# A graph network's kernel on one core: the search's loads and products moved, masks of the real columns alone, two parts finished together, and another last stage

## The chip, the cores and the metric

The kernel runs on one core of one Trainium2 chip. A core has a matrix engine (PE; its weight loads are listed as PEld), a vector engine (DVE), a scalar engine (ACT), GpSimd (POOL), and SyncE (SP), which here only issues transfers. They run their own instruction streams and wait for one another on semaphores. The metric is the device time of one execution in microseconds (us); lower is better. The median of the runs shown is what the prediction is about.

## What is computed

Input: x of 2500 nodes x 256, 40000 edges sorted by destination (denser at low numbers), and the weights of four blocks, each added to its normalized input:

```python
h = max(layernorm(x), 0); x = x + gat(gat(h))       # 8 heads of 32, leaky_relu, softmax over a node's edges
h = max(layernorm(x), 0); x = x + h @ W             # W: edge weights set at [src, dst], the last one of a cell wins
h = max(layernorm(x), 0); x = x + sage_and_dense(h) # three neighbour means, three dense layers
h = max(layernorm(x), 0); x = x + elu(elu(gat4(h))) # 4 heads of 64, exp(-leaky_relu), rows and columns swapped
```

An attention head is worked as a dense product: the edges are first turned into a matrix C of counts (source x destination), and a mask "score above zero" splits C in two, so that the leaky exponential factors into two products of a row term and a column term.

## The kernel before

NT = 20 tiles of 128 nodes hold the 2500 nodes; the last 60 columns of the last tile are padding.

**The count matrix (lines 439 to 612).** The edges lie in 313 chunks of 128. For each of NW = 40 ranges of 64 destinations the chunks that reach into it are taken, in groups of U3 = 3 (387 chunks in all here; 20 ranges have only six chunks, 12 have nine, the first has 54). Per chunk DVE makes two one-hot matrices, `ohc` (line 558) and `ohl` (line 560), in a ring of three; PE multiplies them in three products into `acc` (line 596). Before a slot is used again DVE waits for `s_used`. ACT copies the finished range from `acc` to C (line 542) and prepares `near`, which DVE compares with, for the range after next (line 518). In each range there is also one step of a search for the edges of a cell that are not its last: SP loads rows of keys to `right` and `left` (lines 508, 510), PE makes two products into `psD` (lines 604, 606), ACT squares and clips them (lines 532, 536) and GpSimd scatters the weights (line 423). The body of PE for a range is: the search's products, the first three chunks, the loop over the rest. SP's program starts with nine other loads: x (2.4 MB), its tail, two weight matrices, four attention vectors, a bias (lines 493 to 499); then come the key rows, each waiting until the search before has been done.

**An attention (lines 630 to 1215; three of them).** After the projection and a preparation of factors, a loop over heads `h` and parts `p` of the destination columns makes masks and products. The first two attentions have 8 heads and 2 parts of W = 1280 columns; the third (`split`) has 4 heads and 4 parts of 640. In a part there are 20 steps `s`, one for each source tile. A step is: ACT makes `Rm` = Relu(row term + column bias) (line 1067), DVE takes M = min(Rm, C) (line 1111), PE multiplies M and C with the value matrices (lines 1198 to 1208). With two parts, every fourth step has no ACT operation: DVE compares and multiplies by itself (line 1114); the set `MORE_ON_ACT` gives one such step in each part back to ACT. With four parts, 12 of the 20 steps have a second DVE product Mn (line 1101). Rm and M are rings of SG = 4 slots (5 in the third). After LEAD steps of a part (4; 7) the part before is evacuated: ACT copies the low halves from PSUM to `tl` (line 1075), and DVE puts its stages one by one between its masks: add (line 1138), two scalings by `F2` and `F1` (1142, 1143), their sum `q1` (1147), weight (1152), inverse (1156), mean (1160), and with two parts and p = 1 a copy out of `stash` (1165).

**The last stage (`elu`, lines 1217 to 1308, called on line 2235).** Two ELUs, one on the other, over five batches of four tiles: DVE makes minimum and maximum, ACT the exponential of 1024 columns, DVE the sum, and again. GpSimd issues the load of `xr`, the residual, in one transfer (line 2225), and the output, one transfer for each batch (lines 2230, 2232).

## Time and profile before

| | us |
|---|---|
| median of 3 runs | 2196.62 (2195.84 to 2196.69) |
| the profiled execution | 2193.83 |
| its span in the trace | 2192.2 |
| stage of the count matrix | 33 to 347 |
| masks and products of attention 1 | 421 to 767 |
| of attention 2 | 842 to 1188 |
| of attention 3 | 1877 to 2150 |
| last stage, with the end | 2150 to 2192.2 |

Busy shares of the span: PE 80%, DVE 74%, ACT 64%, POOL 14%. In a row of the timeline stand the start, the duration, the engine, the line, the operation, output<-input with their shapes and count, and in brackets how long the engine stood idle before it and who released it. Rows with x2 or more are merged. Instructions of DVE and ACT overlap by some 0.09 us, so that the distance of two starts is smaller than a duration. Stages between 1188 and 1877 us (the second and third block) are not touched by the change.

### The profile page before, as it was taken

To read this page: it belongs to the slowest core of one execution; us is meant where nothing else is said; L and a number is where in the kernel's file an instruction comes from. 1 tells how busy PE (TensorE), PEld (TensorE's weight loads), DVE (VectorE), ACT (ScalarE), POOL (GpSimd) and SP (SyncE) were. 2 spreads that over 40 slices of the span, in tenths; PEclk is the share of its full clock that TensorE was granted. 3 is DMA by queue.
4 is the path that set the end of the run, shared out by engine and by line. 5 is a ranking of instruction groups with operands and counts; after the bars stand their busy time and mean duration, and the time that the engine had idled before them with its cause. 6 is when DMAs were issued, how large, how long until landed. Compare 5 with 4: busy or idle time off the path is not lost. (4 is left out here: it accounts for less than half of the span.)

```text
span 2192.2 us, 64066 instructions
## 1 busy us (share of the span) xinstructions
PE 1747.3 (80%) x21987; PEld 1343.4 (61%) x21987; DVE 1618.4 (74%) x3673; ACT 1410.0 (64%) x2346; POOL 299.0 (14%) x457
## 2 busy tenths in 40 slices
PE   2998886298998855989885499998989984688881
PEld 1333334288888735888884356665548973688881
DVE  4988877899999978999999722222332257899997
ACT  0146675799999849999996712221213355899992
POOL 2465500466400011000000000000000001000000
PEclk9999998699999987999998799999999997899996
DMA  3000000010110000101011110000001010000102
GB/s 85 1 1 2 2 2 1 27 39 26 38 38 27 14 26 16 38 27 39 26 38 35 67 42 1 0 0 7 1 21 33 22 56 13 14 20 21 27 15 95
DMA packets 32298, 54.99 MB, mean 25 GB/s; under 512 B 10541, under 2 KB 23626, under 8 KB 31800
## 3 DMA queue, kind: packets, MB, share of 16 engines
q1 hardware_dynamic: 27848, 46.45, 6.5%
q0 software_dynamic: 4208, 5.24, 0.7%
q8 instruction: 160, 2.62, 0.5%
q14 instruction: 82, 0.67, 0.1%
HBM read 43.19 MB, written 8.49 MB: 24 GB/s over the span
## 5 line engine op out<-in xcount | busy, mean ns | idle before, releaser
L1198 PE MATMUL ps<-R,M 128*128 128x132 f16 (+1 forms) x8640 | 808.8, 221 | 202.7 <-DVE M L1111 101.9
L1067 ACT ACTIVATE Rm<-rows,cB 128x1280 bf16<-128x1280 f32 (+1 forms) x832 | 884.3, 1153 | 20.3 <-DVE Mn L1101 13.8
L1198 PEld LDWEIGHTS ps<-R,M 128*128 128x128 f16 x8640 | 728.8, 97 | 245.6 <-issue 115.2
L1206 PE MATMUL ps<-HB,C 128*128 128x66 f16 x6400 | 596.1, 193 | 0.0
L1111 DVE TENSOR_TENSOR M<-Rm,C 128x1280 f16<-128x1280 bf16 (+1 forms) x832 | 555.3, 691 | 41.0 <-ACT Rm L1067 37.4
L1206 PEld LDWEIGHTS ps<-HB,C 128*128 128x128 f16 x6400 | 571.7, 97 | 0.0
L1630 PE MATMUL psA<-R,C 128*128 128x512 f16 (+1 forms) x1200 | 253.0, 350 | 20.3 <-POOL ones L1664 9.5
L558 DVE TENSOR_SCALAR ohc<-cells,near 128x1280 f16<-128x1280 f16 x387 | 213.2, 551 | 58.4 <-PE acc L596 54.8
L596 PE MATMUL acc<-ohc,ohl 128*128 128x420 f16 (+1 forms) x1161 | 244.2, 348 | 1.6 <-DVE ohl L560 0.4
L1114 DVE SCALAR_TENSOR_TENSOR M<-rows,cN,C 128x1280 f16<-128x1280 f32 x128 | 197.9, 1546 | 0.0
L1630 PEld LDWEIGHTS psA<-R,C 128*128 (+1 forms) x1200 | 118.7, 99 | 117.5 <-issue 33.2
L596 PEld LDWEIGHTS acc<-ohc,ohl 128*128 128x128 f16 x1161 | 89.9, 98 | 148.6 <-DVE ohl L560 94.1
L423 POOL DMA_INDIRECT wd<-wv,wi x104 | 123.2, 1185 | 128.3 <-issue 71.6
L542 ACT ACTIVATE C<-acc 128x420 f16<-128x420 f32 (+1 forms) x120 | 55.7, 542 | 125.0 <-PE acc L596 125.0
L1781 DVE TENSOR_SCALAR rdeg<-psD 128x1 f32 (+1 forms) x20 | 3.2, 158 | 153.0 <-ACT tl L1746 153.0
L560 DVE TENSOR_SCALAR ohl<-lows,bT 128x128 f16<-128x128 f16 x387 | 101.5, 262 | 0.0
L1560 ACT ACTIVATE R<-L 128x256 f32 (+3 forms) x40 | 14.5, 363 | 129.8 <-DVE L L1792 80.3
L1101 DVE TENSOR_TENSOR Mn<-C,M 128x640 f16<-128x640 f16 x192 | 93.5, 487 | 0.6
L1201 PE MATMUL ps<-VS,C 128*128 128x130 f16 x640 | 88.7, 222 | 0.0
L1198 PE MATMUL ps<-R,Mn 128*128 128x130 f16 x960 | 86.8, 220 | 0.0
L1754 ACT ACTIVATE hT<-ps,b0c 128x128 f32<-128x128 f32 x80 | 22.9, 368 | 86.9 <-PE ps L1705 86.9
L1705 PE MATMUL ps<-xT,W 128*128 128x128 f32 x640 | 76.3, 278 | 1.6 <-ACT xT L1750 1.6
(300 smaller groups left out, 2333.9 us busy)
## 6 DMA issues: line engine op xcount, KB each, us to landing
rows<-rowd SPq DMA_DIRECT2D x32, 640.0 KB, 3.9
rows<-rowd SPq DMA_DIRECT2D x16, 320.0 KB, 3.5
xd<-R SPq DMA_DIRECT2D x4, 640.0 KB, 2.9
xr<-xd SPq DMA_DIRECT2D x20, 128.0 KB, 2.0
xd<-HB SPq DMA_DIRECT2D x1, 2560.0 KB
xr<-xd POOLq DMA_DIRECT2D x1, 2560.0 KB, 9.2
R<-in_x SPq DMA_DIRECT2D x1, 2432.0 KB
xr<-in_x SPq DMA_DIRECT2D x19, 128.0 KB, 2.0
```

What stands on the lines that cost most here:

```text
L423: g.indirect_dma_start(out=wd[:, :], out_offset=bass.IndirectOffsetOnAxis(ap=m["wi"][w][:, :], axis=0), in_=m["wv"][w][:, :], in_offset=No ...
L558: v.tensor_scalar(ohc[:, u, :], cells[:, :], near[:, q % 2, ds(k, 1)], None, ALU.is_equal).then_inc(s_oh, 1)
L560: v.tensor_scalar(ohl[:, u, :], lows[:, :], bT[:, ds(k, 1)], None, ALU.is_equal).then_inc(s_oh, 1)
L596: ins = pe.matmul(bank(b, q % 2), ohl[:, u, :], ohc[:, u, d0 * NT:d1 * NT], start=first_, stop=True, skip_group_check=True)
L1067: a.activation(Rm[:, s % SG, :], rows[:, p % 2, :], ACT.Relu, bias=cB[:, ds(h + s * nh, 1)]).then_inc(s_R, 1)
L1101: v.tensor_tensor(Mn[:, u, :], Cs, M[:, u, :], ALU.subtract).then_inc(s_Mn, 1)
L1111: v.tensor_tensor(M[:, u, :], Rm[:, u, :], Cs, ALU.min).then_inc(s_M if s in ONE else s_cut, 1)
L1114: v.scalar_tensor_tensor(M[:, u, :], rows[:, p % 2, :], cN[:, ds(h + s * nh, 1)], Cs, ALU.is_gt, ALU.mult).then_inc(s_M, 1)
L1198: m = pe.matmul(region(p % 2, r), lhsT, rhs, start=first, stop=True, skip_group_check=True)
L1201: m = pe.matmul(region(p % 2, r), C[:, s * NP + p * W + (r % TP) * P:][:, 0:P], VS[:, TURNED.index(s), :, ds(h * cw, cw)], start=False, st ...
L1206: m = pe.matmul(both[:, :, cw:2 * cw], C[:, s * NP + p * W + r * P:][:, 0:P], VP[:, s, :, ds(h * cw, cw)], start=False, stop=True, skip_gr ...
L1630: m = pe.matmul(psA[:, :], lhsT, SPv[:, s, :, :].rearrange("p l c -> p (l c)"), start=s == 0, stop=s == NT - 1)
```

## The change

- **Keys first.** SP issues the key rows of ranges 0 and 1 first, then the nine other loads, then the key rows of range 2 and on.
- **Three chunks ahead.** In PE's body of a range the first three chunks stand before the search's products.
- **Shorter masks.** In the last part of a head the masks are made over 1220 of 1280 columns (580 of 640). The products still read 1280; the padded rows' factors become zero, by two more small operations of DVE in the preparation.
- **One step from ACT to DVE.** `MORE_ON_ACT` loses (1, 11).
- **Joint finishing.** `tl` holds two parts. After an even part only the add is done; after an odd one add, one scaling of both parts by `F12` (both factors in one operation), one sum, one weight, one inverse, one mean. `stash`, its copy and `q1` are gone. PE's next part waits for the add and no longer for the sum; ACT's copy to `tl` waits for `s_fin`, the mean of the pair before. In the third attention the order of the ten regions in PSUM alternates the two sides.
- **Another last stage.** Ten pairs of tiles. ACT makes e = Relu(-x), e = exp(-e), e = exp(e - 1), each over 512 columns, one pair apart; DVE makes max(e - 1, x) and adds the residual. SP loads the residual in five transfers and writes the output in ten, and the last rows in one more.

```diff
-MORE_ON_ACT = {(0, 7), (1, 11)}
+MORE_ON_ACT = {(0, 7)}
@@ SP, count matrix
-                rows_in(sp, XB, x, s_x)
-                for l, (Wx, gat) in enumerate(((Wx0, gat0), (Wx1, gat1))):
+                def later_loads():
+                    rows_in(sp, XB, x, s_x)
+                    ...
+                    if q == 1:
+                        later_loads()
@@ PE, count matrix
+                    three(0, True)
+
                     with pe.Fori(0, turns) as i:
                         n = turns * q + i
                         pe.wait_ge(s_sq, n + 1)
...
-
-                    three(0, True)
                     with pe.Fori(1, threes) as i:
@@ preparation
+                        for q in (tt, tt2):
+                            ch(v.tensor_scalar(q[:, TH - nh:TH], q[:, TH - nh:TH], padneg[:, 0:1], None, ALU.add))
@@ ACT and DVE, masks
+                    wide = lambda p: W - (NP - N if p == PARTS - 1 else 0)
-                                    a.activation(Rm[:, s % SG, :], rows[:, p % 2, :], ACT.Relu,
+                                    a.activation(Rm[:, s % SG, 0:wide(p)], rows[:, p % 2, 0:wide(p)], ACT.Relu,
@@ evacuation
-                            hold(a, s_E, q + 2)
+                            hold(a, s_fin, h * (PARTS // 2) + p // 2 + 1)
-                                ch(v.tensor_tensor(xv, xv, factor(F2), ALU.mult))
-                                ch(v.tensor_tensor(q1[:, :, :], xu, factor(F1), ALU.mult))
+                                ch(v.tensor_tensor(both(tl), both(tl), factors, ALU.mult))
-                                v.tensor_tensor(q1[:, :, :], q1[:, :, :], xv, ALU.add).then_inc(s_E, 1)
+                                ch(v.tensor_tensor(both(tl)[:, :, 0], both(tl)[:, :, 0], both(tl)[:, :, 1], ALU.add))
+                            return [add] + ([scale, total, weight, inverse, mean] if p % 2 else [])
-                                        side = r // TP if split else 0
+                                        side, d = (r % 2, r // 2) if split else (0, r)
@@ last stage
+                def negative(k):
+                    if k >= 4:
+                        a.wait_ge(s_u, k - 3)
+                    a.activation(e(k), of_heads(k), ACT.Relu, scale=-1.0).then_inc(s_r, 1)
+                def power(k):
+                    a.wait_ge(s_r, k + 1)
+                    a.activation(e(k), e(k), ACT.Exp, scale=-1.0).then_inc(s_e, 1)
+                def again(k):
+                    a.wait_ge(s_e, k + 1)
+                    a.activation(e(k), e(k), ACT.Exp, bias=minus[:, 0:1]).then_inc(s_ee, 1)
...
+                def unit(k):
+                    v.wait_ge(s_ee, k + 1)
+                    v.scalar_tensor_tensor(y(k).rearrange("p (h c) -> p h c", c=64), e(k), -1.0, of_heads(k), ALU.add,
+                                           ALU.max).then_inc(s_u, 1)
+                def residual(k):
+                    v.wait_ge(s_u, k + 1)
+                    if 2 * k % TB == 0:
+                        v.wait_ge(s_xr[2 * k // TB], 16)
+                    v.tensor_tensor(y(k), y(k), xr[:, 2 * k * D:(2 * k + 2) * D], ALU.add).then_inc(s_y, 1)
```

## Rows read from the trace of the kernel before

**Rows 1.** Busy times by stage: window, length, then engines with counts, PEclk, DMA, GB/s.

```profile
33.00:347.00 314.00, 269.63 (x1241) 97.32 (x1241) 257.90 (x790) 160.44 (x519) 129.10 (x257) 1.00 0.05 13
...
421.00:767.00 346.00, 305.37 (x6400) 289.10 (x6400) 334.09 (x488) 335.80 (x320) 102.44 (x120) 0.98 0.09 29
```

**Rows 2.** Timeline, first us of the count matrix: SP's loads, first products, DVE's wait.

```profile
30.85 0.40 SPq L161 DMA_DIRECT2D R<-in_x  x1
...
39.71 0.32 SPq L508 DMA_DIRECT2D right<-flat  x1
...
45.98 0.59 PE L604 MATMUL psD<-notlater,big 128*128 128x512 f16 x1 [26.32 <-DMA left<-flat]
...
48.55 0.55 DVE L558 TENSOR_SCALAR ohc<-cells,near 128x1280 f16<-128x1280 f16 x1 [13.34 <-PE acc L596]
```

**Rows 3.** Timeline at the start of a range of six chunks, all engines.

```profile
331.15 0.30 PEld L596 LDWEIGHTS acc<-ohc,ohl 128*128 128x128 f16 x3 [0.33 <-DVE ohl L560]
...
331.44 0.56 DVE L558 TENSOR_SCALAR ohc<-cells,near 128x1280 f16<-128x1280 f16 x1 [0.34 <-PE acc L596]
...
332.48 0.10 PEld L604 LDWEIGHTS psD<-notlater,big 128*128 128x128 f16 x1 [1.03 <-issue]
...
333.14 1.39 PEld L596 LDWEIGHTS acc<-ohc,ohl 128*128 128x128 f16 x9 [0.23 <-issue]
...
333.16 0.25 DVE L560 TENSOR_SCALAR ohl<-lows,bT 128x128 f16<-128x128 f16 x1
...
334.15 0.55 DVE L558 TENSOR_SCALAR ohc<-cells,near 128x1280 f16<-128x1280 f16 x1 [0.74 <-PE acc L596]
```

**Rows 4.** Groups by line and shape, 360 to 1200 us: busy us, mean ns, idle before.

```profile
L1111 DVE TENSOR_TENSOR M<-Rm,C 128x1280 f16<-128x1280 bf16 x512 | 406.1, 819 | 21.3 <-ACT Rm L1067 19.0 <-PE ps L1206 0.4
...
L1114 DVE SCALAR_TENSOR_TENSOR M<-rows,cN,C 128x1280 f16<-128x1280 f32 x128 | 197.9, 1546 | 0.0
...
L1067 ACT ACTIVATE Rm<-rows,cB 128x1280 bf16<-128x1280 f32 x512 | 647.0, 1361 | 2.7 <-DVEq L1090 2.2
```

**Rows 5.** Timeline of one head in attention 1 (merged rows).

```profile
639.99 0.49 DVE L1142 TENSOR_TENSOR tl<-tl,F 128x330 f32<-128x330 f32 x1
...
659.28 1.03 DVE L1138 TENSOR_TENSOR tl<-ps,tl 128x198 f32<-128x198 f32 x4
...
657.01 20.31 ACT L1067 ACTIVATE Rm<-rows,cB 128x1280 bf16<-128x1280 f32 x16
...
677.43 0.91 ACT L1075 ACTIVATE tl<-ps 128x198 f32<-128x198 f32 x4
...
682.12 0.50 DVE L1142 TENSOR_TENSOR tl<-tl,F 128x330 f32<-128x330 f32 x1
```

**Rows 6.** Groups by line and shape, 1900 to 1965 us in attention 3.

```profile
L1111 DVE TENSOR_TENSOR M<-Rm,C 128x640 f16<-128x640 bf16 x80 | 37.2, 486 | 1.6 <-ACT Rm L1067 1.6
...
L1067 ACT ACTIVATE Rm<-rows,cB 128x640 bf16<-128x640 f32 x81 | 60.2, 821 | 2.8 <-DVE Mn L1101 2.1
```

**Rows 7.** Timeline of attention 3: DVE's wait for ACT, and one part's length.

```profile
2048.04 0.49 DVE L1111 TENSOR_TENSOR M<-Rm,C 128x640 f16<-128x640 bf16 x1 [0.46 <-ACT Rm L1067]
...
2050.18 0.49 DVE L1142 TENSOR_TENSOR tl<-tl,F 128x325 f32<-128x325 f32 x1
...
2066.42 0.49 DVE L1142 TENSOR_TENSOR tl<-tl,F 128x325 f32<-128x325 f32 x1
```

**Rows 8.** Groups by line and shape of the last stage, 1870 to 2192 us.

```profile
L1308 ACT ACTIVATE e<-e 128x1024 f32<-128x1024 f32 x10 | 10.5, 1055 | 28.0 <-DVE e L1262 16.3 <-DVE e L1272 11.8
...
L1291 DVE SCALAR_TENSOR_TENSOR R<-e,R 128x1024 f32<-128x1024 f32 x5 | 6.1, 1225 | 0.5
```

**Rows 9.** The chain that ended last: start us, us, what.

```profile
2151.95 9.24 DMA xr<-xd
...
2187.14 0.59 POOL out L2232
```

**Rows 10.** Timeline of a preparation: one product of DVE while POOL works.

```profile
396.39 1.57 DVE L852 TENSOR_TENSOR F<-HB,U 128x528 f32<-128x528 f32 x1
```

More of the change, by code:

```diff
@@ L1140, in scale @@
+                                for r, n, part in parts:
+                                    ins = v.tensor_tensor(tl[:, p % 2, r:r + n, :], part, tl[:, p % 2, r:r + n, :], ALU.add)
+                                    if r + n < RG:
+                                        ch(ins)
+                                ins.then_inc(s_E, 1)
                             def scale():
+                                hold(v, s_E, q + 3)
                                 ch.wait()
-                                ch(v.tensor_tensor(xv, xv, factor(F2), ALU.mult))
@@ L1159, in mean @@
                                 ch.wait()
-                                ch(v.tensor_tensor(o, q1[:, :, 0:dh], rec[:, :].unsqueeze(2).to_broadcast([P, TP, dh]),
-                                                   ALU.mult))
-                            def unstash():
-                                ch.wait()
-                                ch(v.tensor_copy(room[:, 0:TP, ds(h * cw, dh)], stash[:, :, :]))
-                            stages = [add, scale, both, weight, inverse, mean]
-                            return stages, [unstash] if not split and p == 1 else []
+                                v.tensor_tensor(room[:, some, ds(h * cw, dh)], both(tl)[:, :, 0, 0:dh],
+                                                rec[:, :].unsqueeze(2).to_broadcast([P, 2 * TP, dh]), ALU.mult).then_inc(s_fin, 1)
+                            return [add] + ([scale, total, weight, inverse, mean] if p % 2 else [])
                         def rest(h, p, before):
-                            stages, last = evacuation(*before) if before else ([], [])
-                            steps(h, p, LEAD, NT, stages + last)
+                            steps(h, p, LEAD, NT, evacuation(*before) if before else [])
                         body = parts_in_order(v, steps, rest)
                         with v.Fori(1, nh) as h:
-                            ch.begin(h - 1, PARTS * (NB + 5) + (0 if split else 1))
+                            ch.begin(h - 1, PARTS * (NB - 1) + PARTS // 2 * 4)
                             body(h, False)
                             ch.end(nh - 1)
-                        stages, last = evacuation(nh - 1, PARTS - 1)
-                        for stage in stages + last:
+                        for stage in evacuation(nh - 1, PARTS - 1):
                             stage()
```

198 lines of the change are left out of this document (72 added, 126 removed).

## The prediction

> **What bounds the kernel now.** I read the page's busy shares first (PE 80%, DVE 74%, ACT 64%): no engine is full over the whole span, so the stages have to be read one by one. The table by stage gives the two kinds that matter. In the count matrix DVE is busy for 257.9 of 314 us and in an attention's masks DVE for 334.1 and ACT for 335.8 of 346 us [rows 1]. The reader is to see that in the attention both are full, and that the chunks of the count matrix are paced by DVE with holes in it. The timelines tell what ends those holes: a wait of 13.3 us at the start, behind key rows that come late [rows 2], and one of about 0.7 us in each range [rows 3]. In the last stage the chain of waits alternates between DVE's operations of 1.2 us and begins with a 9.2 us transfer [rows 9]. PE is not the limit in the masks: it is released by DVE, and no part of this change gives it less to do.
>
> **Keys first.** SP issues its first load at 30.85 us and the first key row at 39.71; the products start at 45.98, and DVE, whose ring of three is full, goes on at 48.55 after 13.34 us [rows 2]. In the new order the key rows are issued after some 1.7 us of register work, at about 32.5, and land by about 35.5 (an estimate: the last of three issues at about 33.5 and 2 to 3 us of way, while nothing else is in flight). Since three chunks stand before the search, PE needs no key row for the first of them: it starts at about 34.0, when the first one-hots are ready. It then works at the lower of its two clocks, as it does now at 45.98, where a search's product takes 0.59 us [rows 2], and a chunk takes about 1.05 instead of 0.53. DVE's fourth chunk starts at about 35.5 instead of 48.55, minus 13.0; the search's products then come at the low clock behind the third chunk and cost 0.6 us there. Net **-12.4**. The nine loads are now behind the key rows of range 1, which wait for search 0; they are issued by about 46, in a first range that lasts to about 70. The rows of range 2 are queued behind them on SP and are wanted only after that. Nobody needs x, the weights or the bias before the stage's end. They are free; if the cover were gone, they would cost their 9 us again.
>
> **Three chunks ahead.** This is the part that is easy to believe in and that I price low. A chunk costs DVE 0.55 + 0.25 us less two overlaps of 0.09, so 0.63 [rows 3]. It is ready for PE 0.78 after its start. PE's first product of it at 333.14 releases DVE at 334.15, so 1.02 later. Three chunks of DVE are 1.88: slack 1.88 - 0.78 - 1.02 = 0.08. So every delay of PE beyond 0.08 us stops DVE. Before: the last chunk of the old range starts on PE at 331.15; register work and a load from the table follow, the search starts at 332.48 and the new chunk at 333.14, though it was ready at 332.22 (331.44 + 0.78): late by 0.92, and DVE, which could have gone on at 333.32, starts at 334.15, 0.83 lost [rows 3]. After: the first chunk starts at about 332.2, in time. But behind the third (ready at 333.47, loads until 333.77) come 0.48 us of registers, 0.34 to the second product, and about 0.5 to the next chunk, since the loop's entry now lies there: it starts at 335.1 and was ready at 334.1. Late by 1.0, lost 0.9. The gap is moved, not covered. In the 20 ranges with more than six chunks that is 0.07 worse each, +1.4. In the 20 with six, the loss falls on the next range's first chunk, where DVE has 0.43 us of its own register work (0.34 idle and the missing overlap [rows 3]); the two now run together, 0.9 instead of 1.26, but then PE's own sequence is the bound (3 x 0.53 + 1.6 + 3 x 0.53, less what overlaps, about 4.8 instead of 5.05 a range): -0.25 each, -5. Registers that overlap with running products would help everywhere: with 0.3 us less per range the sum is -17; with 0.2 more it is +3. I take **-5**. Behind the later search stand ACT's squares, its copy of the range and `near`; ACT needs about 4.5 us for a short range, so it fits in 4.8 but would hold at that. The POOL scatter's final step starts 0.2 later against DVE's end: nothing.
>
> **Shorter masks.** 1280 to 640 columns costs ACT 1361 - 821 = 540 ns, 0.84 a column, and DVE 819 - 486 = 333, 0.52 a column [rows 4, 6]. Sixty columns less: ACT 0.051, DVE 0.031, and 0.06 for the one-source mask at 1.0 a column.
>
> **The two attentions of 8 heads.** Now: a head takes 682.12 - 639.99 = 42.13 us; ACT's sixteen steps take 20.31 less one overlap and its copies 0.77, which twice is 42.1 [rows 5]. So ACT is the bound; DVE's own sum is 32 x 0.737 + 8 x 1.464 + 6.1 of evacuation = 41.4. After, part 0: ACT 16 x 1.266 + 0.77 = 21.03. DVE 16 x 0.737 + 4 x 1.464 + 0.95 for the add [rows 5] + the joint stages. A product of 330 elements has an interval of 0.41 and grows by 1.04 ns an element (the 198 against the 66 of the adds), so 1320 elements cost 1.45, the sum of 660 0.76, weight and inverse 0.28, the mean of 640 0.74, together 3.23: in all 21.83. Part 1: ACT 15 x 1.215 + 0.77 = 19.0; DVE 15 x 0.706 + 5 x 1.40 + 0.95 = 18.55. The two engines are now bound in turn: DVE in part 0, ACT in part 1. The sum of the longer ones is 40.83; the longer of the two sums is 40.4. With four slots ACT can't save up part 0's surplus for part 1, so I take the first and 0.12 for the handing over: 40.95, 1.18 less a head, 9.4 in eight. The last evacuation of an attention stands alone and is longer by 1.0 (3.2 instead of 2.1 after the add, with tails). **-8.4 each, -16.8.** Ends: -13 each (a ring that evens out all) and -3 (0.7 lost at each handing over). The wait for `s_fin` looks back a whole part and is met long before.
>
> **The third attention.** A part takes 2066.42 - 2050.18 = 16.24 us, and DVE waits 0.46 for ACT in it [rows 7]. ACT alone is 20 x 0.735 + 0.75 = 15.45, DVE 20 x 0.405 + 12 x 0.402 + 2.7 = 15.6. After: DVE 12.9 + 0.94 + 3.1 = 17.0 in every second part, ACT 15.45 in the others: 32.45 a pair, where it is 32.48 now. **The joint finishing brings nothing here**, since it bunches DVE's work; only the shorter part 3 (20 x 0.051 of ACT) is left, 4 x 1.0, less 1.0 at the end and some handing over: **-2**, between -15 (sums evened out) and +1. The order of the regions gives PE the same products, behind the same waits: nothing.
>
> **Preparation.** Two operations and a wait on DVE's chain, about 0.27 us each time: **+0.8**.
>
> **The last stage.** Now it is 2151.4 to 2192.2, with the last issue at 2187.14, 5.06 before the end [rows 9]. After: ACT has three operations of 512 columns a pair. 1024 columns take 1.055 [rows 8]; less 512 x 0.85 that is 0.62, interval 0.53, 0.6 with a bias from memory. Ten pairs: 30 operations, 16.5 us. DVE: two of 512, from 1.225 at 1024 [rows 8] 0.69, interval 0.61, so 1.2 a pair: hidden behind ACT's 1.65. ACT waits for a memset of POOL, so starts at 2152.2 and ends at 2168.7; the last two of DVE end at 2170.3, SP issues the last rows at about 2171.0, and with the same 5.06 the span ends at 2176.1: **-16.1**. The residual's first quarter lands at about 2156 when the first unit is ready; before, everything waited for the whole, to 2161.2 [rows 9]. Ends: -18 and -12 (each operation without overlap).
>
> The outputs go in twice as many transfers. From the last issue to the end of the span it is 4.5 us, and the 2560 KB of the residual move in 9.24, so 0.92 for each 256 KB [rows 9]. If the ten only queue for the bytes, they are hidden in ACT's pace of 1.65. If each waited for the one before to land, ten of up to 4.5 us would end some 25 us later. I take the first, since the residual's bytes flow without such gaps. The Trainium skill (DMA: Bandwidth & Descriptors, Anatomy of one DMA) gives a transfer 2.0 us and its bytes at 436 GB/s; ten in series would by that be 26 us, some 8 us later than the sum has it.
>
> A product of 330 elements in rows of 33 takes 0.49 us [rows 5], which is 0.15 and 1.04 ns an element. By the Trainium skill (Vector Engine (DVE) Microarchitecture Reference, section 5.2) pairs of words that start on an odd word stream at 1.30 ns a column and others at 1.05; rows of 33 and 65 start so every second time, which would add up to 0.2 us to each joint product, 4 us in all. By that rule the trace disagrees, and the sum goes by the row.
>
> **Sum.** -12.4 - 5 - 16.8 - 2 + 0.8 - 16.1 = -51.5. On the profiled execution's 2193.83 (span 2192.2 and 1.6 around it) that is 2142.3; the median of the runs lies 2.8 above the profiled one, so **2145**.
>
> **The rivals.**
> - *The search's gap is only moved.* PE's register work isn't shared with DVE's and the ranges cost +3: 2153. For it: slack of only 0.08 us. Chance 0.2.
> - *The rings even everything out*, and PE's registers overlap: -17 for the ranges, -13 twice, -9 for the third attention: 2145 - 12 - 9 - 7 = 2117; half of that 2131. For it: DVE and ACT now wait little [rows 4, 5]. Chance 0.15.
> - *The joint stages starve the rest.* 4.2 us of DVE in six steps against rings of four and five; all three attentions give nothing: 2145 + 19 = 2164. Against: in part 0 ACT is 0.8 below DVE anyway. Chance 0.12.
> - *Outputs one after another*: up to 25 us, half of it as the likelier price, 2157. For it: the end of a transfer costs more than its bytes. Against: the one long transfer shows no gaps. Chance 0.05.
> - *Slower than before.* The joint product, with a pattern of three strides and a broadcast, streams slower. A product of 528 elements took 1.57 us once, beside POOL's [rows 10], 3 ns an element; at that rate 1320 take 3.9, 2.5 more, and there are 24 of them, +60, with 8 more for sum and mean: 2213. It decides from 3.2 us a product on. Against: POOL makes no such operations in these loops. Chance 0.01.
>
> **How the numbers follow.** The forecast, 2145 (own range 2137 to 2152), has 0.47. The range 2124 to 2163 takes in half of the gaining rival's way and most of the starving one. A measurement of this kernel can tell about 0.2%, 4.4 us, from no change. Faster 0.98, same 0.01, slower 0.01.
>
> **What the profile will show.** DVE's first wait in the count matrix gone (13.3 to about 1) and the stage some 17 us shorter; DVE's wait per range not at its fourth chunk but at its seventh, about 0.9; short ranges 4.8 us. Heads of 41 us in attentions 1 and 2, with parts of about 21.8 and 19.2; pairs of parts in the third near 32.4. A last stage of some 25 us, ACT full. Wrong if the ranges shrink by more than 0.4 us each, if a head falls below 40.5, or if the joint product takes other than 1.4 to 1.6.

## The result

The changed kernel takes 2129.01 us (median of 4 runs, 2125.31 to 2130.65) against 2196.23 for the kernel before on the same chip (4 runs, 2193.71 to 2196.69): a ratio of 0.9694, 95% interval 0.9677 to 0.9711, 67 us less. The forecast was 2145 with a range of 2124 to 2163. The sign and the range hold; the gain was 15.7 us larger than the sum of the steps. The profiled execution took 2128.39 us with a span of 2126.6, 65.6 less than before. So of the 16 us between 2145 and 2129, 14.1 lie in the stretches below; the prediction had also added 2.8 us from the profiled execution to the median, where it was 0.6 this time.

The stages end in barriers, so the gain can be taken apart by the starts of DVE's operations in both timelines:

| stretch | before | after | change | forecast |
|---|---|---|---|---|
| start to DVE's seventh chunk | 51.4 | 39.1 | -12.3 | -12.4 |
| seventh chunk to the last (387th) | 288.6 | 270.2 | **-18.4** | **-5** |
| last chunk to the first preparation | 45.4 | 44.4 | -1.0 | 0 |
| three preparations of the factors | 114.7 | 115.9 | +1.2 | +0.8 |
| masks of attention 1 | 343.6 | 333.4 | -10.3 | -8.4 |
| masks of attention 2 | 343.0 | 333.4 | -9.6 | -8.4 |
| between attentions 1 and 2 | 40.1 | 40.4 | +0.3 | 0 |
| second and third block, not touched | 652.2 | 656.4 | +4.1 | 0 |
| masks of attention 3 | 270.8 | 268.4 | -2.4 | -2 |
| last stage, with the end | 42.4 | 25.1 | -17.3 | -16.1 |

One term is far off, the ranges of the count matrix. The others are within 2 us of their forecast, and an untouched stretch took 4 away.

**Start of the count matrix.** Timeline of SP, PE and DVE, 30 to 40 us, after; it answers to [rows 2].

```profile
32.03 0.33 SPq L510 DMA_DIRECT2D right<-flat  x1
32.47 0.71 SPq L512 DMA_DIRECT2D left<-flat  x2
...
39.38 0.43 SPq L161 DMA_DIRECT2D R<-in_x  x1
```

```profile
33.58 3.38 PE L600 MATMUL acc<-ohc,ohl 128*128 128x440 f16 x9 [14.35 <-DVE ohl L564]
36.76 0.63 PE L610 MATMUL psD<-notlater,big 128*128 128x512 f16 x1
```

```profile
35.10 0.55 DVE L562 TENSOR_SCALAR ohc<-cells,near 128x1280 f16<-128x1280 f16 x1 [0.33 <-PE acc L600]
...
39.08 0.55 DVE L562 TENSOR_SCALAR ohc<-cells,near 128x1280 f16<-128x1280 f16 x1 [1.25 <-PE acc L600]
```

The key rows are issued at 32.03 instead of 39.71. Three chunks fill PE from 33.58 to 36.8, and the search follows without a wait, so its keys were there. The 13.34 us are gone; 1.25 us are left at the seventh chunk, behind the two products of the search, which take 0.63 and 0.60 instead of the 0.38 that they take later. The prediction called this the lower clock. Only the durations say so: the profile gives a granted clock of 1.00 there (33 to 41 us, and 45 to 52 in the kernel before).

**A range of six chunks.** Timeline of PE's loads and DVE, 286 to 290 us, after; it answers to [rows 3].

```profile
286.41 0.30 PEld L600 LDWEIGHTS acc<-ohc,ohl 128*128 128x128 f16 x3 [0.33 <-DVE ohl L564]
...
286.91 0.10 PEld L610 LDWEIGHTS psD<-notlater,big 128*128 128x128 f16 x1 [0.20 <-issue]
...
287.27 0.09 PEld L612 LDWEIGHTS psD<-right,left 10*128 10x128 f16 x1 [0.27 <-issue]
...
287.59 1.38 PEld L600 LDWEIGHTS acc<-ohc,ohl 128*128 128x128 f16 x9 [0.23 <-DVE ohc L562]
...
288.67 0.55 DVE L562 TENSOR_SCALAR ohc<-cells,near 128x1280 f16<-128x1280 f16 x1 [0.44 <-PE acc L600]
...
289.44 0.30 PEld L600 LDWEIGHTS acc<-ohc,ohl 128*128 128x128 f16 x3 [0.46 <-DVE ohl L564]
```

Before the search's first load PE's loads stood still for 1.03 us [rows 3]; now it is 0.20. The third chunk's loads end at 286.71 and the fourth chunk's begin at 287.59: 0.88 us, where the prediction had 0.48 + 0.34 + 0.5 = 1.32. PE's control instructions (register work, loops and waits; the timeline leaves them out) tell why. The entry of the search's loop and its wait values take from 286.41 to 286.91, 0.50 us, but they begin with the third chunk's loads and not behind them, so that only 0.20 stands alone. The next range's first chunk (289.44) waits for DVE: PE's control instructions are through at 289.24, the load from the table (288.72 to 289.03) among them.

DVE starts a chunk 0.63 us after the one before when nothing holds it. The table has what comes on top at three places of a range, in the mean of the ranges of that size:

| ranges | kernel | first chunk | fourth | seventh |
|---|---|---|---|---|
| of six chunks | before | 0.48 | 0.79 | |
| | after | 0.51 | 0.02 | |
| of nine | before | 0.49 | 0.73 | 0.01 |
| | after | 0.41 | 0.08 | 0.42 |

In a six-chunk range the late search now falls on the first chunk of the next range, where DVE stands still anyway: around the 0.44 us in the row at 288.67 DVE's own control instructions fill the time from 287.62 to 288.61. In a nine-chunk range it falls on the seventh chunk, and 0.42 is left there.

ACT is now full in the short ranges as well. Its timeline, 283.5 to 288.2 us:

```profile
283.67 0.60 ACT L536 ACTIVATE junk<-psD 128x512 f32<-128x512 f32 x1
284.53 0.40 ACT L540 ACTIVATE junk<-junk,oob 128x128 f32<-128x128 f32 x1 [0.26 <-ACT junk L536]
...
286.08 1.35 ACT L546 ACTIVATE C<-acc 128x440 f16<-128x440 f32 x3
287.33 0.61 ACT L522 ACTIVATE near<-codeT,base 128x384 f32<-128x384 f32 x1
287.95 0.60 ACT L536 ACTIVATE junk<-psD 128x512 f32<-128x512 f32 x1
```

From one square of the search to the next (287.95 - 283.67 = 4.28) it stops only once, for 0.26 us behind its own square. In the kernel before it also waited 0.7 to 0.9 us for the others in most such ranges.

**One head of attention 1.** DVE's adds, one row of four in each part, its joint product, and ACT's masks of the same head; they answer to [rows 5].

```profile
599.82 1.03 DVE L1146 TENSOR_TENSOR tl<-ps,tl 128x198 f32<-128x198 f32 x4
621.47 1.03 DVE L1146 TENSOR_TENSOR tl<-ps,tl 128x198 f32<-128x198 f32 x4
640.66 1.03 DVE L1146 TENSOR_TENSOR tl<-ps,tl 128x198 f32<-128x198 f32 x4
```

```profile
601.50 1.53 DVE L1154 TENSOR_TENSOR tl<-tl,F 128x1320 f32<-128x1320 f32 x1
642.34 1.52 DVE L1154 TENSOR_TENSOR tl<-tl,F 128x1320 f32<-128x1320 f32 x1
```

```profile
610.81 7.48 ACT L1075 ACTIVATE Rm<-rows,cB 128x1280 bf16<-128x1280 f32 x6 [0.66 <-DVE M L1120]
618.53 0.91 ACT L1083 ACTIVATE tl<-ps 128x198 f32<-128x198 f32 x4 [0.24 <-PE ps L1209]
619.30 18.30 ACT L1075 ACTIVATE Rm<-rows,cB 128x1220 bf16<-128x1220 f32 x15
```

The part with the joint steps takes 21.65 us and the other 19.19, together 40.84. In the first ACT waits (0.66 and 0.24), so DVE sets its length; in the second ACT's fifteen masks stand without a gap. The joint product takes 1.53 us.

**Last stage.** Timeline after, from its first instruction to the last issue; it answers to [rows 8, 9].

```profile
2103.33 1.15 ACT L2163 ACTIVATE R<-HB 128x512 f32<-128x512 f32 x2 [6.87 <-POOL minus L2142]
...
2115.85 0.70 ACT L2171 ACTIVATE R<-R,minus 128x512 f32<-128x512 f32 x1
2116.46 0.61 ACT L2163 ACTIVATE R<-HB 128x512 f32<-128x512 f32 x1
...
2118.63 1.32 ACT L2171 ACTIVATE R<-R,minus 128x512 f32<-128x512 f32 x2
...
2121.26 1.29 DVE L2191 TENSOR_TENSOR R<-R,xr 128x512 f32<-128x512 f32 x2
2122.96 0.36 SPq L2154 DMA_DIRECT2D out<-R  x1
```

ACT works from 2103.33 to 2119.95 without a gap, 16.6 us. DVE ends 2.6 us behind it, and the span ends 3.6 behind the last issue.

### The profile page after: what moved, and what is told of

It reads as the page before. It is cut to its first block and busy times, and to the rows that moved or that the text cites. A ratio compares the mean times of both kernels' runs of the same rounds, so it can differ in the third digit from the quotient of the medians.

```text
span 2126.6 us, 63582 instructions
## 1 busy us (share of the span) xinstructions
PE 1734.2 (82%) x21987; PEld 1347.7 (63%) x21987; DVE 1582.6 (74%) x3455; ACT 1379.3 (65%) x2350; POOL 305.1 (14%) x451
## 5 line engine op out<-in xcount | busy, mean ns | idle before, releaser
L1201 PE MATMUL ps<-R,M 128*128 128x132 f16 (+1 forms) x8640 | 826.8, 221 | 190.5 <-DVE M L1120 112.3
L1201 PEld LDWEIGHTS ps<-R,M 128*128 128x128 f16 x8640 | 762.8, 97 | 219.7 <-issue 115.3
L1075 ACT ACTIVATE Rm<-rows,cB 128x1280 bf16<-128x1280 f32 (+3 forms) x816 | 846.9, 1131 | 32.1 <-DVE Mn L1110 18.8
L1209 PE MATMUL ps<-HB,C 128*128 128x66 f16 x6400 | 590.0, 193 | 0.0
L1120 DVE TENSOR_TENSOR M<-Rm,C 128x1280 f16<-128x1280 bf16 (+3 forms) x816 | 532.5, 678 | 37.1 <-ACT Rm L1075 29.7
L1123 DVE SCALAR_TENSOR_TENSOR M<-rows,cN,C 128x1280 f16<-128x1280 f32 (+1 forms) x144 | 217.7, 1512 | 0.0
L423 POOL DMA_INDIRECT wd<-wv,wi x104 | 127.2, 1223 | 131.2 <-issue 68.9
L1201 PE MATMUL ps<-R,Mn 128*128 128x130 f16 x960 | 127.3, 221 | 0.0
L1204 PE MATMUL ps<-VS,C 128*128 128x130 f16 x640 | 119.8, 223 | 0.0
L1201 PEld LDWEIGHTS ps<-R,Mn 128*128 128x128 f16 x960 | 93.4, 97 | 0.0
L1110 DVE TENSOR_TENSOR Mn<-C,M 128x640 f16<-128x640 f16 (+1 forms) x192 | 92.1, 480 | 0.6
```

Of the source, the lines that this page charges most:

```text
L423: g.indirect_dma_start(out=wd[:, :], out_offset=bass.IndirectOffsetOnAxis(ap=m["wi"][w][:, :], axis=0), in_=m["wv"][w][:, :], in_offset=No ...
L1075: a.activation(Rm[:, s % SG, 0:wide(p)], rows[:, p % 2, 0:wide(p)], ACT.Relu, bias=cB[:, ds(h + s * nh, 1)]).then_inc(s_R, 1)
L1110: v.tensor_tensor(Mn[:, u, 0:wide(p)], Cs, M[:, u, 0:wide(p)], ALU.subtract).then_inc(s_Mn, 1)
L1120: v.tensor_tensor(M[:, u, 0:wide(p)], Rm[:, u, 0:wide(p)], Cs, ALU.min).then_inc(s_M if s in ONE else s_cut, 1)
L1123: v.scalar_tensor_tensor(M[:, u, 0:wide(p)], rows[:, p % 2, 0:wide(p)], cN[:, ds(h + s * nh, 1)], Cs, ALU.is_gt, ALU.mult).then_inc(s_M, 1)
L1201: m = pe.matmul(region(p % 2, r), lhsT, rhs, start=first, stop=True, skip_group_check=True)
```

## Experiments

Every kernel was timed beside the kernel before (2195.96 to 2196.34 us in the three groups). Since the stages are apart, a stretch of the profile tells more than the median. Most stretches of one kernel agree to 0.5 us from one profile to the next, the untouched block excepted. Over all changed kernels whose code is the same there, the masks and the last stage keep close to that, and the stretch of the ranges lies between 269.5 and 270.2; but the start up to the seventh chunk lies between 38.4 and 39.4, and the stretch from the last chunk to the first preparation between 44.2 and 45.7.

### The search ahead of the chunks again

```diff
-                    three(0, True)
                     with pe.Fori(0, turns) as i:
                         ... the search's two products
+                    three(0, True)
                     with pe.Fori(1, threes) as i:
```

> The changed kernel with the search's products put back ahead of the range's first three chunks; everything else stays, the keys first too. Theory A (the gain of the ranges comes from the new order, because PE's register work and its load from the table at a range's start then lie behind products and beside DVE's own boundary work): DVE's fourth chunk starts some 2.5 us later than 35.10, since PE now waits for the key rows, and the six-chunk ranges go back from 4.28 to 5.0 us and the nine-chunk ones from 6.7 to 7.0; DVE's last chunk ends 17 + 2 = 19 us later, and the run takes 2148 us. Theory B (my reckoning on record: the gap is only moved, -5 for the ranges; the other 12 us that the stage gained come from the early keys in some way that I haven't seen): the ranges give back 5 and the start 2, so 2136 us.

Measured: 2147.91 us, ratio 0.9775 (0.9759 to 0.9792). DVE's seventh chunk starts at 39.6, and from there to the last it takes 288.55 us, to a tenth what it took before (288.6); between two searches 5.03 us in the mean of the 19 six-chunk ranges, where the changed kernel has 4.36, and 6.96 in twelve long ones against 6.64. DVE's fourth chunk starts 1.7 us later (36.83), where theory A had 2.5. So theory A holds: the whole of the 18.4 us comes from the three chunks ahead, and the keys alone are worth 51.4 - 39.6 = 11.8. The group of the search's first loads (39 to 309 us) shows where it lies, first this kernel, then the changed one:

```profile
L608 PEld LDWEIGHTS psD<-notlater,big 128*128 128x128 f16 x35 | 3.3, 96 | 35.7 <-issue 35.7
```

```profile
L610 PEld LDWEIGHTS psD<-notlater,big 128*128 128x128 f16 x39 | 3.7, 96 | 8.3 <-issue 8.1
```

An idle time of 1.02 us ahead of each search has become 0.21.

### The load from the table behind the third chunk

```diff
                     threes = threes_of(coming)
-                    if q + 1 < NW:
-                        coming = packed(pe, q + 1)
                     ...
                     three(0, True)
+                    if q + 1 < NW:
+                        coming = packed(pe, q + 1)
```

> The changed kernel with one edit: PE loads the next range's entry of the table behind the three opening chunks, just ahead of the search, instead of ahead of them. Same instructions, same number. Theory A (what counts is only the register work between the third chunk and the fourth; what stands at the range's start is free): the load and its registers, 0.3 us of PE's busy time and up to 0.45 with what hangs on it, are now in the one stretch that has no cover, so 40 ranges lose 0.3 to 0.45 each: +12 to +18, about 2143 us, and the PE idle time ahead of the search's first load rises from 0.20 to 0.5 or 0.65 in every range. Theory B (the sequencer works ahead of the products, so no place costs more than another): 2129 us, no change.

Measured: 2137.96 us, ratio 0.9733 (0.9717 to 0.9749). The stretch of the ranges is 280.7 instead of 270.2, +10.5: 0.26 a range. That is theory A's direction, and theory B falls; but the loss is under the +12 to +18 that theory A expected, and the run is 5 us under its 2143. Six-chunk ranges take 4.59 (+0.23), the twelve long ones 6.94 (+0.30). The idle time ahead of the search rises from 0.20 to 0.55 and chunk four comes 1.20 us behind the third's loads:

```profile
287.20 0.30 PEld L598 LDWEIGHTS acc<-ohc,ohl 128*128 128x128 f16 x3 [0.33 <-DVE ohl L564]
288.05 0.10 PEld L610 LDWEIGHTS psD<-notlater,big 128*128 128x128 f16 x1 [0.55 <-issue]
288.38 0.09 PEld L612 LDWEIGHTS psD<-right,left 10*128 10x128 f16 x1 [0.24 <-issue]
288.70 1.39 PEld L598 LDWEIGHTS acc<-ohc,ohl 128*128 128x128 f16 x9 [0.23 <-issue]
```

The same instructions at two places: behind the third chunk they cost 0.26 us a range more than at its start. That answers what the order does. At the range's start DVE has its own boundary work, and PE would wait for it anyway. By the Trainium skill (Perfetto Trace Analysis, Sequencer Loop) a sequencer pushes engine instructions into a queue and executes control instructions itself. This trace agrees: the load from the table (0.30 us) starts at 287.20, together with the third chunk's loads, and the search comes 0.55 us behind their end.

### The keys late again

```diff
+                later_loads()
                 sp.sem_inc(s_D, 1)
                 ...
-                    if q == 1:
-                        later_loads()
```

> The changed kernel with the nine loads of features, weights, score vectors and bias issued ahead of the first key rows again; three chunks still stand ahead of the search. The key rows come at 39.7 and the search's first product at about 46, as in the kernel before; but chunks one to three are now multiplied before that, so DVE makes chunks four to six at once and stops at its seventh. Theory A (the two parts overlap): DVE's seventh chunk starts at about 48.5 instead of 39.1, so +9.4 and 2138.5 us. Theory B (the parts are worth what the sum on record has, each by itself): +12.4, 2141.5 us.

Measured: 2138.73 us, ratio 0.974 (0.9723 to 0.9756). DVE's timeline:

```profile
37.12 0.55 DVE L561 TENSOR_SCALAR ohc<-cells,near 128x1280 f16<-128x1280 f16 x1 [0.35 <-PE acc L599]
...
48.64 0.55 DVE L561 TENSOR_SCALAR ohc<-cells,near 128x1280 f16<-128x1280 f16 x1 [10.80 <-PE acc L599]
```

The seventh chunk starts at 48.64, theory A's 48.5: +9.5, and the rest of the ranges is as in the changed kernel (269.5). Theory B's +12.4 falls. Beside the new order the keys are worth 9.5, by themselves 11.8: three chunks ahead would have covered 2.8 of the wait.

### Masks of the full width

```diff
-                    wide = lambda p: W - (NP - N if p == PARTS - 1 else 0)
+                    wide = lambda p: W
```

> The changed kernel with every mask 1280 (or 640) columns wide again, the joint finishing kept. Theory A (an attention's part takes the longer of what ACT and DVE need in it): the second part of a head in attentions 1 and 2 loses 15 x 0.051 on ACT and 15 x 0.031 + 5 x 0.06 on DVE, 0.77 either way, so a head takes 41.6 instead of 40.85 and the two attentions 12 us more; the third loses 20 x 0.051 in one part of four, 4 us: 2145 us. Theory B (it is the joint finishing that shortened the heads, and the rings even out a mask's 0.05): under 5 us in all, 2133.

Measured: 2140.68 us, ratio 0.9751 (0.9734 to 0.9767). The masks take 338.3, 338.2 and 272.3 us: +4.9, +4.9 and +3.8, 13.6 in all, where theory A had 16. A head is 41.45 us (21.72 and 19.73), 0.60 longer where theory A had 0.77; theory B, under 5 in all, falls. ACT's mask costs 1363 ns at 1280 columns and 1313 at 1220 (groups by shape of the changed kernel, 438 to 683 us), the 0.05 of the prediction.

### Attentions 1 and 2 finished part by part

```diff
+                APART = not split
                 ...
+                            if APART:
+                                return [add, scale, total, weight, inverse, mean, unstash]
                             return [add] + ([scale, total, weight, inverse, mean] if p % 2 else [])
```

> The changed kernel with attentions 1 and 2 finishing each part by itself, as the kernel before did (the first part's result waits in a buffer and is copied with the second's), the third jointly. By the rows of the changed kernel DVE's work in a head grows by two small products, sums, weights and means for one large of each (0.06 to 0.2 us each) and the copy of 0.25: 0.65 in all, to 41.05; by parts 21.0 (ACT) and 20.4 (DVE), 41.4. Theory A (the longer engine of each part): a head of 41.1 to 41.4 instead of 40.85, so +4 to +9 us in both and about 2135. Theory B (bunching costs what the fewer operations save): 40.85 and 2129.

Measured: 2135.54 us, ratio 0.9726 (0.9709 to 0.9742). With the copy at the end the masks take 337.3 and 337.2 us, +3.9 and +3.8. DVE's adds of one head:

```profile
602.97 1.03 DVE L1151 TENSOR_TENSOR tl<-ps,tl 128x198 f32<-128x198 f32 x4
623.84 1.03 DVE L1151 TENSOR_TENSOR tl<-ps,tl 128x198 f32<-128x198 f32 x4
644.30 1.03 DVE L1151 TENSOR_TENSOR tl<-ps,tl 128x198 f32<-128x198 f32 x4
```

20.87 and 20.46, 41.33 a head, at the upper end of theory A, that is the sum of the longer engine in each part (21.0 and 20.4). Theory B falls, and the rule that the prediction had weighed against this one, that the longer of the two engines' sums over a head sets it, is 0.3 too short: DVE's sum was put at 41.05 here, and at 40.4 for the changed kernel (40.84 measured). The joint form is worth 0.5 us a head here.

### The third attention finished part by part

The same edit with `APART = split`, for the third attention alone (no copy is needed there).

> The changed kernel with the third attention finishing each part by itself (a product of 650 elements, a sum of 325, weight, inverse and mean of 320 in every part), the first two jointly as now. The joint form saves DVE about 0.55 us a pair of parts but sets 3.1 us of work into one part and none into the other. Theory A (prediction on record: the longer engine of each part decides): DVE 12.9 + 0.94 + 1.83 = 15.7 in every part, ACT 15.45, so a pair takes 31.4 to 32.4 instead of 32.7: the third attention takes 258 to 267 us instead of 268.4, and the last finishing is 1.0 shorter. Theory B (the rings of five carry the bunched work over the part's end): the 0.55 a pair come back, +4 us, 272.5.

Measured: 2125.56 us, ratio 0.9681 (0.9665 to 0.9698). The masks take 266.3 instead of 268.4 us. DVE's adds at the start of the attention, first the changed kernel (every second part is 2 us longer), then this one:

```profile
1854.36 1.02 DVE L1146 TENSOR_TENSOR tl<-ps,tl 128x195 f32<-128x195 f32 x4
1869.51 1.02 DVE L1146 TENSOR_TENSOR tl<-ps,tl 128x195 f32<-128x195 f32 x4
1886.51 1.02 DVE L1146 TENSOR_TENSOR tl<-ps,tl 128x195 f32<-128x195 f32 x4
```

```profile
1852.05 1.02 DVE L1151 TENSOR_TENSOR tl<-ps,tl 128x195 f32<-128x195 f32 x4
1868.11 1.02 DVE L1151 TENSOR_TENSOR tl<-ps,tl 128x195 f32<-128x195 f32 x4
1883.75 1.02 DVE L1151 TENSOR_TENSOR tl<-ps,tl 128x195 f32<-128x195 f32 x4
```

32.15 a pair jointly, 31.70 apart: here the joint form loses 0.45 in the first pair, and 0.34 to 0.36 in four others, though it has fewer operations. But two of the pairs are 2 to 3 us longer in either form (see the last section), and over the seven pairs between the first and the last add the gain is 1.2 us. From the first mask to the last it is 0.4 us, within what such a stretch varies by; the other 1.7 of the 2.1 come from the last finishing, which stands alone and is shorter for one part than for two (7.1 against 8.8 us from the last mask on). The medians (2125.6 against 2129.0) are at the edge of what they can tell. Theory B's +4 falls, and theory A is at the low end of its gain (266.3 in a forecast of 258 to 267).

### The joint steps spread over two parts

```diff
+                        LATER = 4 if split else 1
                         ...
+                            now = evacuation(*before) if before else []
+                            if before and before[1] % 2:
+                                now, left_over[:] = now[:-LATER], now[-LATER:]
+                            steps(h, p, LEAD, NT, now)
                         ...
+                        def first_steps(h, p, s0, s1):
+                            now, left_over[:] = left_over[:], []
+                            steps(h, p, s0, s1, now)
```

> A new variant: the changed kernel, but the last steps of a joint finishing run among the first masks of the next part instead of in the same part: in attentions 1 and 2 the mean alone (0.74 us), in the third sum, weight, inverse and mean (1.8 us). No instruction is added or removed. Theory A (the longer engine of each part decides): attentions 1 and 2 have DVE at 21.1 and 19.3 and ACT at 21.0 and 19.0, so a head of 40.4 instead of 40.85, -7 us in both; the third has DVE at 15.3 and 15.5 and ACT at 15.45, a pair of 31.1 to 32.2 instead of 32.7, -4 to -12 us: together 2110 to 2118 us. Theory B (the rings already carry half a microsecond over a part's end): no change, 2129. Theory C (ACT's copies of a part's accumulators wait for the mean, and moving it later holds ACT up): slower than 2129.

Measured: 2116.31 us, ratio 0.9641 (0.9625 to 0.9657): **12.7 us better than the changed kernel**, with not one instruction more or less. The masks take 330.1, 330.1 and 263.7 us: -3.2, -3.3 and -4.8, together 11.3. DVE's adds of one head:

```profile
596.63 1.03 DVE L1146 TENSOR_TENSOR tl<-ps,tl 128x198 f32<-128x198 f32 x4
618.15 1.03 DVE L1146 TENSOR_TENSOR tl<-ps,tl 128x198 f32<-128x198 f32 x4
636.99 1.03 DVE L1146 TENSOR_TENSOR tl<-ps,tl 128x198 f32<-128x198 f32 x4
```

21.52 and 18.84, 40.36 a head where theory A had 40.4. Only the sum tests it: the adds stand four masks into a part, so the mean that was moved over the part's start still lies between the same two adds. Since DVE and ACT do the same work as in the changed kernel, a rule that goes by an engine's sum over a head would have given no change. In the third attention a pair takes 31.75 (1844.95 to 1876.70), inside its 31.1 to 32.2. Theories B and C fall. The untouched block was 0.8 shorter too, and 1.2 of the 13.5 us by which the span shrank lie ahead of the first masks.

### The old last stage

The function `elu` and its call as before, behind everything else of the changed kernel.

> The changed kernel with the last stage of the kernel before (DVE alone for all but the exponentials, the residual in one load, five outputs from GpSimd's queue). From the end of the third attention's last DVE operation to the end of the span it took 42.4 us before and takes 25.1 now. Theory A (the stages stand alone behind a barrier): the stage is 42.4 again, +17.3, 2146 us. Theory B (part of that difference comes from what the attention leaves behind, for instance a queue still at work): +14 to +16.

Measured: 2146.38 us, ratio 0.9773 (0.9757 to 0.979). From the end of attention 3 to the end of the span it is 42.3 us, against 25.1: 17.2, theory A. Theory B's 14 to 16 falls: the stage stands alone.

### The search's first product ahead of the chunks

On top of the spread steps:

```diff
+                    landed = pe.snap(pe.to_reg(turns * (q // 2 * 48) + 48), min_val=48, max_val=48 * NW * RND)
+                    pe.wait_ge(s_sq, turns * q + 1)
+                    same_edges()
                     three(0, True)
-                    with pe.Fori(0, turns) as i:
                     ...
+                    hold(pe, s_row[q % 2], landed)
+                    search()
+                    with pe.If(turns - 1):
                         ...
```

> The variant of e6_spread with one more edit in the count matrix: of the search's two products the first, which needs no key row, stands ahead of the three opening chunks, and only the second stays behind them; the wait values are worked out ahead of the opening chunks too, and the second turn of a search stands under a condition instead of in a loop. Theory A (each tenth that PE spends between the third chunk and the fourth is a tenth that DVE loses, and PE's work at a range's start is covered): the product's interval of 0.31 leaves that stretch in 40 ranges, DVE's wait at the range's end falls from 0.54 to about 0.25, and the stretch from DVE's seventh chunk to its last takes 258 to 262 us instead of 269.7; the run takes 2106 us, against 2116 of e6_spread. Theory B (the condition and the extra registers cost what the product gave, or the product now delays the opening chunks instead): 2116 us or more.

Measured: 2110.45 us, ratio 0.961 (0.9594 to 0.9626), the fastest kernel of this study. But the ranges take 266.3 us instead of 269.7, so -3.4 where theory A had -8 to -12. The medians are 5.9 us apart, the profiled spans only 3.9: the untouched block is 2.0 shorter (653.6 against 655.5), which the edit doesn't touch, and the stretch from the last chunk to the first preparation is 1.6 longer (45.8 against 44.2), where kernels without this edit reached 45.7. Timeline of PE's loads:

```profile
280.49 0.10 PEld L605 LDWEIGHTS psD<-notlater,big 128*128 128x128 f16 x1 [0.60 <-issue]
...
280.71 0.31 PEld L600 LDWEIGHTS acc<-ohc,ohl 128*128 128x128 f16 x3
...
282.46 0.09 PEld L609 LDWEIGHTS psD<-right,left 10*128 10x128 f16 x1 [0.35 <-issue]
...
282.78 1.38 PEld L600 LDWEIGHTS acc<-ohc,ohl 128*128 128x128 f16 x9 [0.23 <-issue]
```

The third chunk's loads end at 282.11 and the fourth's begin at 282.78: 0.67 instead of 0.88. The first product's 0.36 left, and 0.15 came back as idle time ahead of the remaining one (0.35 for 0.20). Against the kernel with the spread steps the nine-chunk ranges gained 0.16 (6.43 against 6.59): what DVE loses at their seventh chunk fell from 0.41 to 0.19. The six-chunk ranges, half of all, gained nothing (4.34 against 4.35). There two other limits stand close together. DVE loses 0.47 at the first chunk, against 0.50 with the spread steps and 0.48 in the kernel before, which is its own boundary work; and ACT's round of a range takes 4.27 to 4.28 us wherever it waits for nobody, in the changed kernel, with the spread steps and here, and it is never shorter except in the last ranges, where `near` is no longer made. The miss was to take the gain in all 40 ranges. And the range's start isn't free without a bound either: PE now stands idle for 0.60 ahead of the first product, and multiplies the first chunk at 280.71, though DVE had it ready at 280.51.

### Both kernels once more

> The kernel before, once more, for the stretch that the change doesn't touch (from the end of the second attention to the third's preparation): 652.2 us in the profile before, 654.0 to 656.6 in seven profiles of changed kernels. Theory A (it varies by itself, with the clock that TensorE is granted and with the arrival of a weight): 652 to 657. Theory B (the change made it longer): 652 again.

> The changed kernel once more, beside the one before on the same chip, for the same stretch: 656.4 us in its first profile. Theory A: anywhere from 652 to 657. Theory B: 654 or more. All other stretches within 0.5 us of the first profile.

Measured: spans 2195.2 and 2126.3 us; the untouched block 654.7 and 656.0. The first is against theory B, the second fits both. So it moves by itself by 2.5 us under the kernel before (652.2, 654.7), and over all profiles of changed kernels it lies between 653.6 and 656.6. The wait that varies, PE's in the third block, in the changed kernel's first profile:

```profile
1222.16 0.39 PE L1540 MATMUL psA<-R,C 128*128 128x512 f16 x1 [3.41 <-DMA b1r<-in_L_gnn_b]
...
1223.00 0.59 PE L1540 MATMUL psA<-R,C 128*128 128x512 f16 x1
```

PE waits 3.41 us for a small weight row, and a microsecond later its products take 0.59 instead of 0.38 for some 3 us, the granted clock being 0.50 from 1223 to 1226, the lower of its two levels. In the kernel before's first profile PE waited 2.38 us there, for DVE, and the granted clock stayed at 1.00; in its second PE waited 1.8 for the weight row. Whether the change adds a microsecond or two here is open; two profiles of the kernel before are too few, and no mechanism was seen.

## Why the prediction was right, and where it was not

- **Keys first: right.** Forecast -12.4, measured -12.3 to the seventh chunk and -13.4 to the fourth. The step "They are free", of the nine loads, held: the stretch behind the last chunk, where they are first used, is 1.0 shorter and not longer.
- **Three chunks ahead: the mechanism was only half right, and its size wrong.** The term that was mis-sized is "0.48 us of registers, 0.34 to the second product, and about 0.5 to the next chunk", behind the end of the third chunk's loads. It is 0.20, 0.36 and 0.32: 0.88 instead of 1.32. The 0.48 was right as a length (0.50), but it was put behind loads that it runs beside. The about 0.5 assumed that the entry of the chunks' loop costs PE time of its own; in fact chunk four follows the second product with 0.23 of idle time, as in [rows 3] (at 333.14), where the search's loop ended but no other began. The sum had a slip too: its own terms, +1.4 and -5, make -3.6, and it took -5. What came: nine-chunk ranges are 0.32 shorter (forecast 0.07 longer) and six-chunk ones 0.68 (forecast 0.25); 12 and 19 of them make 16.8 of the 18.4 us. The verdict "the gap is moved, not covered" was right for the nine-chunk ranges, where DVE loses 0.42 at the seventh chunk instead of 0.73 at the fourth, and wrong for the six-chunk ones: the prediction saw that the late search and DVE's boundary work run together there, but then took PE's own sequence as the bound, at 4.8 us. They take 4.36 in the mean. The 4.5 that it gave ACT is 4.28, and there ACT does hold, as it had said of its own figure. The end of the range at -17, "Registers that overlap with running products", is what came, and 1.4 us more. The prediction's own mark, "Wrong if the ranges shrink by more than 0.4 us each", was crossed (0.46). That the total stayed inside the range is owed to the range, which took in half of the gaining rival's way, and not to this step.
- **Attentions 1 and 2: right.** Parts of 21.8 and 19.2 were forecast, 21.65 and 19.19 measured; a head of 40.95 against 40.84. The rule that each part takes its longer engine was tested from both sides, at 41.33 (forecast 41.1 to 41.4) and 40.36 (forecast 40.4); with full masks it was 0.15 too long (41.45, forecast 41.6). The masks gained 1.2 to 1.9 us more than forecast in each attention, 0.9 of it by the heads.
- **Joint product: right.** 1.53 us in a forecast of 1.4 to 1.6. The slower rival, 3 ns an element, did not show. Nor did the 1.30 ns a column of the Trainium skill (Vector Engine (DVE) Microarchitecture Reference, section 5.2) that was weighed there: from 330 elements at 0.50 us to 1320 at 1.53 it is 1.04 ns an element, for rows of 33; 1300 elements in rows of 65 take 1.51. The Trainium skill has that figure for pairs of words that start on an odd word in both sources; here the rows are long and one source is broadcast, so the trace doesn't speak against it.
- **Attention 3: right, and the sharper claim too.** -2.4 against -2. "The joint finishing brings nothing here, since it bunches DVE's work" is even mild: against finishing part by part it costs 2.1 us, of which 1.7 is the last finishing alone, and the masks' width gives 3.8. Joint, that last finishing is 1.95 us longer than in the kernel before (8.83 against 6.88); the forecast had 1.0.
- **Preparation:** +1.2 against +0.8.
- **Last stage: right.** -17.3 against -16.1. ACT's sixteen and a half us are 16.6. The start was 0.6 earlier and the end 1.4 earlier than forecast, DVE's tail 1.0 longer. The outputs don't queue for one another: ten are issued within 13.3 us and the span ends 3.6 us behind the last issue, so ten in series (25 us) did not come. The 2.0 us a transfer that the prediction set beside that rival is the figure of the Trainium skill (DMA: Bandwidth & Descriptors, Anatomy of one DMA) for transfers that GpSimd issues; SyncE issues these.
- **The rivals.** "The rings even everything out" gave -17 for the ranges, and only that half of it came. "The search's gap is only moved" (+3 for the ranges) fell by their 18.4 us less. "The joint stages starve the rest" fell by the heads, "Outputs one after another" by the last stage, and "Slower than before" by the joint product.

## What to carry to other kernels

Price the register and loop work of an in-order engine by place: where another engine is at its own boundary it can cost nothing, and in a stretch that one with a shallow ring waits for it costs nearly all of itself (0.26 us for one load from a table, moved by three chunks). It runs beside products that are already queued, so count it from the start of their loads and not from their end. When two engines take turns at being the longer one, part by part, the sum of the longer ones is the time: moving a step of 0.7 us over the boundary gained 6.5 us in two attentions, nearly as much as the joint form with its fewer operations (7.7), and joining work that bunches it can lose a little where the parts are short. A place that is free has a bound; work out how much is free before moving a second thing there. And once a wait is gone, look for the engine that was slack beside it: here ACT, whose 4.28 us set the floor of the short ranges for the next change.

## What was not expected of the hardware

- After a wait of 3.41 us PE's clock went to 0.50 for some 3 us within a microsecond of starting again (row at 1223.00), and the untouched block varied by 4.4 us over thirteen profiles (652.2 to 656.6). A gain of a few microseconds is better read from its own stretch than from the medians.
- In the third attention two of the eight pairs of parts take 2 to 3 us longer than the others, in every variant. DVE waits there for ACT at a part's start, and ACT's own wait is put down to a mask that had long been done. In the part-by-part variant:

```profile
1960.82 0.90 DVE L1124 TENSOR_TENSOR M<-Rm,C 128x640 f16<-128x640 bf16 x2 [2.99 <-ACT Rm L1079]
```

  It isn't the row terms: the last ones loaded before it had landed at 1946.56, 12 us before ACT went on at 1958.46. PE's loads stood idle 2.7 us in the same stretch with no releaser, and instruction packets moved in it, as they do in stretches without a stop. That the engines fetch code there is a guess; no run tested it.
